# First stage of a convolution and attention block: tokens turned as two runs side by side, keys and queries stored once

## What is computed

```python
x = x + conv_block(group_norm(x))        # sums of 7 shifted copies, a 5x5 dilated depthwise conv,
                                         # a 1x3 conv t2, a data-dependent 7x1 mixing of t2 by t3 = <shifts of x, x>
t = tokens(x)                            # (16, 3136, 32)
n = layer_norm(t)
q, k, v = n @ Wq + bq, n @ Wk + bk, n @ Wv + bv
t = t + softmax(q @ k.T / sqrt(32)) @ v + n
n = layer_norm(t)
t = t + top2_of_8_experts(n)             # router softmax, two best experts, weighted
```

## Time and profile before

| | us |
|---|---|
| median of 3 runs | 2888.14 |
| lowest, highest | 2882.81, 2888.21 |
| the profiled execution | 2885.98 |
| its span, first to last instruction | 2884.2 |

### The profile page before, as it was taken

The page is one execution under the profiler, slowest core; times in us unless marked ns, Lnnn a source line. Parts: engine busy times, 40 slices in busy tenths (PEclk is TensorE's granted clock), DMA queues, the critical chain, the costliest instruction groups (busy, mean ns, idle before and its releaser), DMA issues. The chain is left out here.

```text
span 2884.2 us, 48428 instructions
## 1 busy us (share of the span) xinstructions
PE 2469.7 (86%) x18630; PEld 992.9 (34%) x18630; DVE 2398.6 (83%) x4268; ACT 1661.1 (58%) x2202; POOL 353.0 (12%) x442
## 2 busy tenths in 40 slices
PE   3877777636999999999999999999999987877776
PEld 2332323211222222222222222222222227666665
DVE  4575758458999999999999999999999946888787
ACT  1243434343777777777777777777777772333322
POOL 0010101110000000000000000000000002554545
PEclk9988889856999999999999999999999995676666
DMA  7775757251011013011011011011010001322220
GB/s 180 181 234 182 225 175 209 79 190 42 1 57 51 7 58 117 1 57 57 1 57 57 1 57 57 1 57 57 14 45 24 24 23 57 102 68 75 93 67 23
DMA packets 58941, 221.00 MB, mean 77 GB/s; under 512 B 15911, under 2 KB 28835, under 8 KB 52067
## 3 DMA queue, kind: packets, MB, share of 16 engines
q1 hardware_dynamic: 54242, 197.61, 22.2%
q0 software_dynamic: 3280, 16.80, 1.6%
q10 hardware_dynamic: 1200, 3.69, 0.4%
HBM read 81.67 MB, written 74.60 MB: 54 GB/s over the span
## 5 line engine op out<-in xcount | busy, mean ns | idle before, releaser
L1229 DVE TENSOR_REDUCE at_XM<-at_psX 128x1 f32<-128x448 f32 x2688 | 1546.3, 620 | 90.0 <-PE at_psX L1092 69.3
L1158 ACT ACTIVATE at_PR<-at_psS 128x896 f32<-128x896 f32 x1344 | 1162.9, 915 | 449.2 <-PE at_psS L1072 447.2
L1110 PE MATMUL at_psV<-at_PR,at_V 128*32 128x448 f32 x5376 | 645.2, 552 | 0.1
L1072 PE MATMUL at_psS<-at_US,at_KS 128*128 128x448 f16 x2688 | 636.1, 356 | 0.6 <-ACT at_PR L1158 0.2
L1092 PE MATMUL at_psX<-at_KS,at_US 64*128 64x448 f16 x1344 | 490.4, 365 | 61.8 <-DVE at_XM L1229 43.0
L1092 PE MATMUL at_psX<-at_KS,at_UH 64*128 64x448 f16 x1344 | 490.4, 365 | 0.0
L1092 PEld LDWEIGHTS at_psX<-at_KS,at_US 64*128 64x128 f16 x1344 | 124.5, 93 | 718.0 <-DVE at_XM L1229 661.9
L1072 PEld LDWEIGHTS at_psS<-at_US,at_KS 128*128 128x128 f16 x2688 | 200.8, 98 | 273.2 <-ACT at_PR L1158 118.6
L1496 POOL TENSOR_TENSOR fi_WE<-fi_WE 128x256 f32<-128x256 f32 (+1 forms) x224 | 212.9, 978 | 172.4 <-DVE fi_WE L1550 171.5
L1207 POOL CAST at_mrow<-at_mt 7x128 f16<-7x128 f32 x64 | 17.9, 279 | 1654.8 <-DVE at_mt L1248 1654.8
L374 PE MATMUL psA<-sb_stacks,sb_lhs 128*32 128x448 f32 x1568 | 178.9, 577 | 25.0 <-DVE sb_X L786 25.0
(11 more groups left out here) (193 smaller groups left out, 2163.5 us busy)
## 6 DMA issues: line engine op xcount, KB each, us to landing
sums<-at_O SPq DMA_DIRECT2D x16, 1568.0 KB, 6.3
fi_SUMS<-sums SPq DMA_DIRECT2D x16, 1568.0 KB, 6.6
sb_stacks<-sb_T SPq DMA_DIRECT2D x64, 270.5 KB, 7.3
sb_stacks<-sb_Xp SPq DMA_DIRECT2D x64, 248.8 KB, 8.5
sb_stacks<-sb_Xp SPq DMA_DIRECT2D x64, 248.0 KB, 5.7
at_KS<-key_stacks SPq DMA_DIRECT2D x16, 784.0 KB, 7.8
at_US<-query_stacks SPq DMA_DIRECT2D x16, 784.0 KB, 10.5
sb_stacks<-sb_T SPq DMA_DIRECT2D x64, 172.5 KB, 6.3
```

Of the source, the lines that this page charges most:

```text
L1072: last = nc.tensor.matmul(psS[:, at % 2, k, 0:TILE], KS[:, b, (2 * c + k) * P:(2 * c + k + 1) * P], US[:, b, t * TILE:(t + 1) * TILE], sta ...
L1110: last = nc.tensor.matmul(psV[C * q:C * q + C, 0:TILE], V[:, b, G * k + q, :], PR[:, (n * 2 * STEPS + 2 * q4 + q // 2) % PRS, q % 2, :], s ...
L1158: nc.scalar.activation(PR[:, f % PRS], psS[:, at % 2, :, 0:TILE], ACT.Exp).then_inc(p_ready, 1)
L1229: nc.vector.tensor_reduce(o, psX[:, (at + j) % 3, 0:TILE], AX.X, ALU.max).then_inc(x_done, 1)
```

## The change

An image's 25 blocks of 128 tokens are laid out as two runs of 13 and 12 (the 26th is zeros). A block j of Y16 holds, side by side, the high and low part of block j and the high and low part of block j + 13. So 13 transposes turn an image, and keys have rows 0 to 63 for the first run and 64 to 127 for the second, with TQ = 1664 columns. Two matrices `mhi` and `mlo`, zero where the two runs would mix, make both runs' queries in 4 tiles of 416 columns, two matmuls each. Keys and queries are stored once, as 128 x 1664.

The doubling is now done by the attention's loads: 19 DMAs per image, 8 for each run and 3 for the values. Queries' rows 32 and 96 are left out, so several of these move 31 rows. Row 32 of US (and row 96 of UH, once) is zeroed by GpSimd, for image 0's buffer by VectorE, and `maxima` of an image's first pair waits for it.

There are two token buffers, so that images 0 and 1 stay in SBUF and two go through HBM; US has its own memory. The order of the step is rewritten on all five engines: image 1 is normalised between the tap rows and turned in the middle of the second half, image 2's centre comes before the new weights, `add` of tiles 0 and 1 before the tap rows 3 and 4, statistics behind image 3's low parts, and normalisation behind add(4).

```diff
-        mstack = sb("mstack", [P, P], F16)
+        mhi, mlo = sb("mhi", [P, P], F16), sb("mlo", [P, P], F16)
...
+            xr = xh.rearrange("p (r j c) -> p r j c", r=2, c=C)
+            y = y16.rearrange("p (j r s c) -> p r j s c", r=2, s=2, c=C)
...
-                for q in range(min(8, NC - 8 * s)):
+                for q in range(min(8, JC - 8 * s)):
...
-                nc.tensor.matmul(psQ[:, (KSETS + i) % 3, 0:TILE], mstack[:], z.KS[:, i * TILE:(i + 1) * TILE],
-                                 start=True, stop=True).then_inc(q_full, 1)
+                o, k = psQ[:, (KSETS + i) % 3, 0:QTILE], z.KS[:, i * QTILE:(i + 1) * QTILE]
+                nc.tensor.matmul(o, mhi[:], k, start=True, stop=False)
+                nc.tensor.matmul(o, mlo[:], k, start=False, stop=True).then_inc(q_full, 1)
...
+                for i in range(3):
+                    conv3(g, i)
+                turn_stack(g, 0, 0)
+                turn_stack(g, 1, 0)
+                correlate(g, 0, 0)
+                turn_stack(g, 2, 0)
+                correlate(g, 1, 0)
+                run(keys_of(0))
+                turn_stack(g, 3, 0)
+                correlate(g, 2, 0)
+                correlate(g, 3, 0)
+                for i in range(3, NT):
+                    conv3(g, i)
+                    run(queries_of(0)[i - 3:i - 2])
+                turn_stack(g, 0, 1)
+                turn_stack(g, 1, 1)
+                correlate(g, 0, 1)
+                run(keys_of(1))
+                turn_stack(g, 2, 1)
+                correlate(g, 1, 1)
+                run(queries_of(1)[0:2])
+                turn_stack(g, 3, 1)
+                correlate(g, 2, 1)
+                run(queries_of(1)[2:4])
+                correlate(g, 3, 1)
...
-                between = {2: keys_of(2), 3: queries_of(2), 5: keys_of(3), 6: queries_of(3)}
+                between = {2: keys_of(2), 3: queries_of(2), 4: keys_of(3), 5: queries_of(3)}
...
-                for s in (0, 2):
-                    nc.scalar.activation(z.Y16[:, :, s, :], z.XH, ACT.Copy).then_inc(y_high, 1)
+                nc.scalar.activation(z.Y[:, :, :, 0, :], z.XR, ACT.Copy).then_inc(y_high, 1)
...
-                link(nc.vector.tensor_tensor(z.Y16[:, :, 1, :], z.XH, z.Y16[:, :, 0, :], ALU.subtract))
-                link(nc.vector.tensor_copy(z.Y16[:, :, 3, :], z.Y16[:, :, 1, :]))
+                link(nc.vector.tensor_tensor(z.Y[:, :, :, 1, :], z.XR, z.Y[:, :, :, 0, :], ALU.subtract))
```

The attention's part:

```diff
-        LOADS = 6
+        LOADS = 19
...
-                for dst, src in ((KS[:, b], scr["ks"][n]), (US[:, b], scr["us"][n]),
-                                 (UH[HALF:P, b], scr["us"][n, 0:HALF]),
+                for r, (a, z) in enumerate(((0, TQ), (TQ, T))):
+                    k = ks[HALF * r:HALF * r + HALF, 0:z - a]
+                    hi, lo = (us[HALF * h + C * r:HALF * h + C * r + C, 0:z - a] for h in range(2))
+                    parts += [(KS[0:HALF, b, a:z], k), (KS[HALF:P, b, a:z], k), (US[0:C, b, a:z], hi),
+                              (US[C + 1:HALF, b, a:z], hi[1:C]), (US[HALF:HALF + C, b, a:z], lo),
+                              (US[HALF + C + 1:P, b, a:z], lo[1:C]), (UH[HALF:HALF + C, b, a:z], hi),
+                              (UH[HALF + C + 1:P, b, a:z], hi[1:C])]
```

More of the change, by code:

```diff
@@ L26 @@
 NP = NC // 2
+JC = NP + 1
+TQ = JC * P
 E = 8
@@ L421, in keys_of @@
                 def keys_of(n):
-                    return [(turn_keys, m, n, s) for s in range(KSETS)] if old else []
+                    return [(turn_keys, m, n, s, first[n]) for s in range(KSETS)] if old else []
                 def queries_of(n):
-                    return [(queries, m, n, i) for i in range(NT)] if old else []
+                    return [(queries, m, n, i, first[n]) for i in range(QSETS)] if old else []
                 def run(parts):
@@ L573, in step @@
+                for i in range(3):
+                    to_t2(g, i)
                 if old:
-                    keys(m, 1)
-                    query_high(m, 1)
+                    squares(m, 0, first[0])
+                turned(g, 0, 0)
                 if old:
-                    squares(m, 2)
-                    deviations(m, 2)
-                    high_parts(m, 2)
-                    keys(m, 2)
-                    query_high(m, 2)
+                    deviations(m, 0)
+                turned(g, 1, 0)
@@ new lines, in step @@
+                if old:
+                    high_parts(m, 0, first[0])
+                turned(g, 2, 0)
+                if old:
+                    keys(m, 0, first[0])
+                turned(g, 3, 0)
+                for i in range(3, NT):
+                    to_t2(g, i)
+                    if old:
+                        query_high(m, 0, (i - 3,), first[0])
+                turned(g, 0, 1, slice(0, 2))
+                if old:
+                    squares(m, 1, first[1])
+                turned(g, 0, 1, slice(2, None))
@@ new lines, in step @@
+                turned(g, 1, 1, slice(0, 2))
+                if old:
+                    deviations(m, 1)
+                turned(g, 1, 1, slice(2, None))
+                if old:
+                    high_parts(m, 1, first[1])
+                    keys(m, 1, first[1])
+                turned(g, 2, 1)
+                if old:
+                    query_high(m, 1, (0, 1), first[1])
+                turned(g, 3, 1)
+                if old:
+                    query_high(m, 1, (2, 3), first[1])
+                    for n in (2, 3):
+                        squares(m, n, first[n])
+                        deviations(m, n)
+                        high_parts(m, n, first[n])
+                        if n == 2:
+                            keys(m, n, first[n])
+                            query_high(m, n, range(QSETS), first[n])
@@ L611, in _, with store_tokens @@
         def _(pool):
-            def store_tokens(m, n, z=first, alone=False):
+            def store_tokens(m, n, z, more):
                 r = m * G + n
@@ L617, in store_tokens @@
                 pool.dma_start(image("val", r), z.XH.rearrange("p k c -> p (k c)")).then_inc(val_out, 16)
-                if n + 1 < G and not alone:
+                if n < 2 and more:
                     if n == 0:
```

306 lines of the change are left out of this document (140 added, 166 removed).

## The result

| | before | after |
|---|---|---|
| median of the runs, us | 2887.26 (4 runs) | 2944.91 (4 runs) |
| lowest, highest | 2882.81, 2888.21 | 2943.33, 2948.2 |
| span of the profiled execution | 2884.2 | 2944.4 |
| mean granted clock of TensorE | 0.898 | 0.881 |

The ratio is 1.0204, with a 95% interval of 1.0187 to 1.0222: the change makes the kernel 58 us slower.

The account below looks back on a forecast made before the run. Order within the step, not work, was taken to bound the first stage, and TensorE the attention. First stage -60, late start +32 and steady loads +8 gave -20: 2866 us, own range 2845 to 2887, widened to 2832 to 2900.

Parts of the forecast that it names:

- The gain of the first stage: Convolution steps and token tail before the attention: less work and a new order save 60 us, bounds -35 and -75.
- The walk through a step: First stage, a step with both groups: the new order followed engine by engine, 146.3 to 125.3 us.
- The half stack: First stage, load of 4.0 MB at 253 GB/s: 16 us, landing 2 us after TensorE wants it.
- the wait for image 0 absorbs that: First stage: TensorE's wait for image 0, about 2.8 us, takes up the half stack landing 2 us late.
- the 2.5 us for the queue: First stage: the next half stack shares the queue with token stores, charged 2.5 us in each of two steps.
- The late start: Start of the attention: slow loads and maximum rows queued behind them make scores begin 32 us later.
- the 27 us of one image on one engine: Attention loads: six 31-row DMAs use one engine, 27 us an image, between 26 and 30.
- +42 at 30 us an image: Start of the attention: upper bound of the delay to the scores, if an image's load takes 30 us.
- The steady part: Attention after its start: maximum rows land slightly late, 0.6 us lost in each of 13 images, +8 us.
- rival D: Attention: load still holds its engine when part 2's maximum rows are issued; +30, 2916 us; slower from 2.2 us an image; chance 0.13.
- rival C: First stage gives half, through waits at keys and a clock staying low after each wait: 2896 us, slower; chance 0.14.
- Rightly at nothing: Attention: GpSimd's added zeroing, VectorE's two row clears and TensorE's new wait for zeroed rows cost nothing.

Follow-up runs that it names:

- e9: On top of e1, ScalarE takes image 0's squares ahead of its first conv3 copy and the square root ahead of the third: 2827.49 us.
- e1: The changed kernel with each of its six 31-row loads cut into 16 and 15 rows, 25 DMAs an image instead of 19: 2837.73 us.
- e4: The changed kernel with only the 31-row load of UH, the copy of the high part, cut into 16 and 15 rows: 2852.22 us.
- e7: The changed kernel with its loads as they are, but the maximum rows' small DMAs issued from GpSimd's queue instead of SyncE's: 2875.15 us.
- e2: The kernel before with only its query-stack loads cut as the change cuts them, 13 DMAs an image instead of 6: 2974.92 us.

## Why the prediction was wrong

**The gain of the first stage: right in kind, 8.5 us less than forecast.** Predicted -60, measured -51.5, inside its bounds of -35 and -75. The walk through a step held. After, in step 2 TensorE waits for VectorE 3.44, 7.61, 0 and 8.23 us before the four images' keys, against 2.8, 7.6, 0 and 7.8, and it doesn't wait before conv5 tile 2. TensorE is busy 98.2 us of that step, against 99, and idle 31.6, against 26; the difference is its stand at conv3. The tail's period is 12.87 us (key stores at 540.33, 553.20, 566.08), against 12.4.

```profile
PE psQ L422 <- DVE sb_Y L770: 19.3, 3, 8.2
...
540.33 0.32 SPq L290 DMA_DIRECT2D key_stacks<-sb_KS  x1
553.20 0.32 SPq L290 DMA_DIRECT2D key_stacks<-sb_stacks  x1
566.08 0.32 SPq L290 DMA_DIRECT2D key_stacks<-sb_stacks  x1
```

Two terms were off. The half stack was given 16 us from issue to landing, from bytes and rate; it took 20.5:

```profile
249.45 11.61 SPq L277 DMA_DIRECT2D sb_stacks<-sb_Xp  x16
...
269.95 6.48 PE L350 MATMUL psA<-sb_stacks,sb_lhs 128*32 128x448 f32 x48 [5.67 <-DMA sb_stacks<-sb_Xp]
```

And "the wait for image 0 absorbs that" looked at VectorE alone: VectorE stood 3.77 us in step 2 for ScalarE's squares behind conv3's copies (e9). Both fall hardest on step 1, which gained 10.3 us and not 16. Its stand at conv3 was foreseen nearly right (2.2 + 3 + 4 = 9 us, measured 10.4), but VectorE lost most of it too, 9.01 us; e9 takes 4.7 us off this step, against e1.

```profile
139.24 6.94 PE L350 MATMUL psA<-sb_stacks,sb_lhs 128*32 128x448 f32 x48 [10.43 <-DMA sb_stacks<-sb_Xp]
...
147.66 0.99 DVE L758 TENSOR_REDUCE sb_lvar<-sb_KS 128x25 f32<-128x800 f32 x1 [9.01 <-ACT sb_KS L523]
```

Stage by stage, with the 2.5 us for the queue in steps 2 and 3: steps 0 and 1 gave -14.0 where -18 was predicted, step 2 -16.5 for -18.5, step 3 -11.2 for -12.5, and the tail up to the first load -9.8 for -11.4.

**The late start: right in kind, 10 us short.** Predicted +32, measured +42.3; the first maxima began 34.0 us after the first load, not 29. The step that failed is the 27 us of one image on one engine. The earlier trace rows has the rate of 31-row loads, 23 GB/s, and the prediction quotes it; 583 KB + 110 KB at 23 GB/s are 30.1 us. It then took a mean with the 26 GB/s that an engine reaches in a full load. An image took 30.2 to 30.7 us: SP reached the values' load of images 0, 1 and 2 at 599.79, 630.44 and 660.66. The upper bound, "+42 at 30 us an image", was the answer.

**The steady part: the term that decided the sign.** Predicted 0.6 us x 13 = 8, measured 68.8. With 27 us the engine was done at 852 and the rows came 0 to 1 us late; with the 30.1 of the row in hand it is done 3 us later, and every one of these goes into TensorE. The prediction had this as rival D with its threshold, 2.2 us an image; measured were thirteen stands of 3.3 us on average, and one of 1.5. Its chance of 13% was too low: the forecast's 0.6 stood on a mid value of a quantity that sat at a threshold and was multiplied by thirteen. Working both terms with 30.1 would have given -60 + 42 + (0.6 + 3.1) x 13 = +30, slower, which is D's own sum. e4 shows the threshold from the other side.

**What no case had: the clock.** Each stand cost TensorE up to 2.3 us more, 24 us in all. TensorE stayed at full clock from 686 to 2371.5 us before, so no row of the attention priced a stand there. But the first stage's rows did show mean clocks of 0.87 beside stands, and rival C spoke of "a clock that stays low after each wait" while D, with thirteen new waits in the kernel's busiest stretch, didn't. D plus the clock is what happened: -51.5 + 42.3 + 44.6 + 24.2 + 0.6 = +60.2.

**Rightly at nothing:** GpSimd's cleared rows, VectorE's two and the new waits. e1 has them all, and its attention takes what the kernel before took: 1671.2 us from first to last half-width score tile, against 1673.2 before. SP's issues for an image had been put at 8 to 20 us (19 x 1.3 are 25); in the steady part they took 25.3 (812.14 to 837.41) and ended 3.4 us before SP issued the rows of part 2, so nothing hung on them there.

## What to carry to other kernels

When a value stands beside a threshold and its cost is multiplied by a loop, work the sum at both ends of the value, and take the rate from the row nearest in shape, not a mean with a better one. A partition count in a DMA is a design choice: 31 rows cost 85 us here that 16 + 16 don't, and when a design leaves one row out, cut the rest into 16 + 15. Small DMAs that an engine waits for shouldn't stand behind bulk loads in one queue; and before a wait is said to absorb a delay, follow that wait's own chain through every engine's order.

## What the runs showed of the hardware

- One queue slows its issuer when it doesn't drain: SP needed 6.2 us for four query loads of 31 and 32 rows after, 1.59 us for the first four on an empty queue, 2.87 us for six of e1's, and could issue the first maximum rows only at 666.37, 83 us after the first load.
- The place in a queue costs more than the engine: small rows from another queue, issued 19.6 us into a load that kept one engine for some 35 us, were usable 5.1 us later (e7), where 4.2 us were enough with the load over.
- TensorE's clock behind a stand in an otherwise full stretch: stands of 0.7 to 1.05 us left it at 1.00 in all thirteen cases of e7; stands of 1.9 to 2.6 us were followed by a mean of 0.66 to 0.70 over five us in ten of thirteen cases of e2; stands of 2.9 to 3.7 us by 0.50 to 0.70 in ten of thirteen cases after. One of 1.5 us after was followed by 0.66, one of 1.0 us in e2 by 1.00. Which stand is followed by a fall isn't settled by its length alone.
